# Ten-fold instead of eight-fold unrolling of the second edge loop of a two-layer graph network, on one core

## The reference

```python
src = edge_index[0]; dst = edge_index[1]               # layer 0: gated attention over all edges
attn = jax.nn.silu(jnp.sum(q[dst] * k[src] * dk, axis=1)) * _cosine_cutoff(edge_weight)
agg = jax.ops.segment_sum(v[src] * dv * attn[:, None], dst, num_segments=N)
...
key_e = k_rel[edge_type, edge_src]                     # layer 1: typed attention, 4 heads of 64
att = (q[edge_dst] * key_e).sum(-1) * rel_pri[edge_type] / sqrt(dk)
seg = edge_dst * r + edge_type
ex = jnp.exp(att - segment_max(att, seg)[seg])
w = ex / segment_sum(ex, seg)[seg]
hsum = segment_sum(w[:, :, None] * val_e, seg)
...                                                    # mean over types, typed projection, skip, norm
```

## Time and profile before

| | us |
|---|---|
| median of 3 runs | 3775.6 (3765.82 to 3777.75) |
| the profiled execution | 3789.33 |
| its span on the core | 3787.5 |
| second edge stage in it | about 1770 to 3450 |

### The profile page before, as it was taken

One profiled execution on the slowest core, in us unless ns is written; L12 is line 12 of the kernel. 1 busy time (PEld: TensorE's weight loads), 2 busy tenths in 40 slices (PEclk: granted clock), 3 DMA queues, 4 the chain that ended last, 5 costly groups with the idle time before them and its releaser, 6 DMA issues. The chain is left out here.

```text
span 3787.5 us, 113336 instructions
## 1 busy us (share of the span) xinstructions
PE 3442.8 (91%) x25474; PEld 2765.5 (73%) x25475; DVE 3283.3 (87%) x10411; ACT 2816.1 (74%) x8685; POOL 2448.1 (65%) x2605
## 2 busy tenths in 40 slices
PE   3978999999999997996999999999999999997997
PEld 2547777777777775774777777777777777776986
DVE  6768999999999995664899998999999999996775
ACT  2856777777777774553889888889889998885553
POOL 2656777777777773554566666666666666663776
PEclk8989999999999998998899999999999999998998
DMA  3879999999999994776888887888888888875664
GB/s 107 255 225 303 296 298 299 298 299 299 294 299 298 295 263 158 262 261 220 234 234 236 236 227 218 231 230 235 230 226 237 236 236 233 231 228 149 214 204 134
DMA packets 613511, 915.39 MB, mean 242 GB/s; under 512 B 210712, under 2 KB 422794, under 8 KB 612916
## 3 DMA queue, kind: packets, MB, share of 16 engines
q0 software_dynamic: 168160, 579.41, 47.9%
q1 hardware_dynamic: 445268, 335.07, 31.9%
HBM read 739.98 MB, written 177.47 MB: 242 GB/s over the span
## 5 line engine op out<-in xcount | busy, mean ns | idle before, releaser
L905 POOL DMA_INDIRECT kv<-kv_table,rec x864 | 887.5, 1027 | 293.6 <-issue 269.9
L1572 POOL DMA_INDIRECT kv1c<-kv_table,rec x912 | 877.4, 962 | 285.4 <-issue 262.4
L1617 ACT ACTIVATE wv<-kv1c,wv 128x64 f32<-128x64 f32 x3648 | 904.0, 334 | 16.0
L1680 DVE CUSTOM_DVE_ANT_0 masked_scores<-score_p,far 126x384 f32<-126x384 f32 x1216 | 604.6, 553 | 62.7 <-issue 28.5
L943 ACT ACTIVATE gates<-gates_p 128x512 f32<-128x512 f32 x864 | 465.5, 591 | 78.9 <-PE gates_p L1074 76.6
L1772 PE MATMUL sum_p<-wv,hot 128*126 128x260 f32 x1824 | 519.7, 424 | 2.3 <-ACT wv L1617 2.3
L1737 PE MATMUL qe_p<-qrel,hotT 126*128 126x256 f32 x1824 | 464.9, 392 | 26.1 <-ACT hotT L1602 18.0
L1094 PE MATMUL sum_p<-msg,hot_weighted 128*126 128x256 f32 x1728 | 432.2, 393 | 5.3 <-ACT hot_weighted L951 5.3
L1737 PEld LDWEIGHTS qe_p<-qrel,hotT 126*128 126x128 f32 x1824 | 363.8, 200 | 88.2 <-ACT hotT L1602 19.3
L1772 PEld LDWEIGHTS sum_p<-wv,hot 128*126 128x126 f32 x1824 | 339.8, 200 | 86.6 <-issue 3.8
L1582 POOL TENSOR_TENSOR faded<-acc,fade 126x260 f32<-126x260 f32 x304 | 189.2, 622 | 329.6 <-ACT fade L1625 324.1
(11 more groups left out here) (285 smaller groups left out, 7230.6 us busy)
## 6 DMA issues: line engine op xcount, KB each, us to landing
key<-segment_keys SPq DMA_DIRECT2D x304, 189.0 KB
q_blk<-q_table SPq DMA_DIRECT2D x216, 256.5 KB
acc_table<-acc SPq DMA_DIRECT2D x304, 128.0 KB
qrel<-q_by_relation SPq DMA_DIRECT2D x304, 126.0 KB
feat<-in_edge_feat_t SPq DMA_DIRECT2D x216, 128.0 KB
agg_and_x_plus_h<-total SPq DMA_DIRECT2D x216, 126.0 KB
kv1c<-kv_table,rec POOLq DMA_INDIRECT x912
kv<-kv_table,rec POOLq DMA_INDIRECT x864
```

The costliest lines, as they stand in the source:

```text
L905: pool.indirect_dma_start(kv[it.slot(AHEAD)][:, t, :], None, c["kv0_d"], bass.IndirectOffsetOnAxis(ap=rec[k][:, t, 0:1].bitcast(I32), axis ...
L1572: pool.indirect_dma_start(kv[k][:, t, :], None, c["kv1_d"], bass.IndirectOffsetOnAxis(ap=rec[k][:, t, 0:1].bitcast(I32), axis=0)).then_inc ...
L1617: ins = act.activation(wv[k][:, t, h, 0:DK], kv[s][:, t, D + h * DK:D + (h + 1) * DK], ACT.Copy, scale=wv[k][:, t, h, DK:DK + 1])
L1680: dve.tensor_tensor_reduce(junk[k][:, h], score_p[:, :, h, :], far[it.slot(4)][:], 1.0, -BIG, ALU.subtract, ALU.max, top[s][:, h:h + 1]).t ...
```

## The change

The loop of `edges_1` gets an unrolling of its own, U1 = 10, and `run_chunks` takes the unrolling as an argument; `edges_0` passes U = 8 as before. Everything in `edges_1` that was U deep is now ten deep, everything four deep is now five deep (`DEEP1`), and every wait for a free buffer looks back ten or five chunks in place of eight or four. The lags and the order of the stage functions stay. Two iterations are still written out ahead of the loop, which are now 20 chunks. `prepare` divides the chunk count by ten with a multiplication by 6554 and a shift by 16. The weights of `nodes_1` now live in a scope that closes before `w2` is allocated, so that their space is free for the deeper buffers.

```diff
+U1, DEEP1 = 10, 5
...
-def run_chunks(eng, steps, stages):
+def run_chunks(eng, steps, stages, unroll):
...
-    for s in range(2 * U):
+    for s in range(2 * unroll):
...
     with eng.Fori(2, steps) as i:
-        for u in range(U):
+        for u in range(unroll):
             for lag, f in stages:
-                f(Item(i, u - lag, U))
+                f(Item(i, u - lag, unroll))
...
+        with ExitStack() as middle:
+            def hold_w1(name, shape):
+                return middle.enter_context(nc.sbuf_tensor(name, shape, F32))
...
+            edges_0(nc, c)
+
+            nc.clear_and_free_semaphores(nc.allocated_since(before))
+            nc.all_engine_barrier()
+            nodes_1(nc, c)
...
-                link(dve.tensor_scalar(total_i[:], total[:], float(U - 1), None, ALU.add))
-                link(dve.tensor_scalar(total_i[:], total_i[:], U.bit_length() - 1, None, ALU.arith_shift_right))
+                dve.tensor_scalar(total_i[:, 0:1], total[:, 0:1], float(U - 1), None, ALU.add)
+                link(dve.tensor_scalar(total_i[:, 1:2], total[:, 1:2], float(U1 - 1), None, ALU.add))
+                link(dve.tensor_scalar(total_i[:, 1:2], total_i[:, 1:2], float((1 << 16) // U1 + 1), None, ALU.mult))
+                dve.tensor_scalar(total_i[:, 0:1], total_i[:, 0:1], U.bit_length() - 1, None, ALU.arith_shift_right)
+                link(dve.tensor_scalar(total_i[:, 1:2], total_i[:, 1:2], 16, None, ALU.arith_shift_right))
...
-        rec = [sb(f"rec1{k}", [P, T1, 4]) for k in range(U)]
+        rec = [sb(f"rec1{k}", [P, T1, 4]) for k in range(U1)]
...
-        kv = [sb(f"kv1c{k}", [P, T1, 2 * D]) for k in range(U)]
-        far = [sb(f"far{k}", [SEG, T1, P]) for k in range(4)]
+        kv = [sb(f"kv1c{k}", [P, T1, 2 * D]) for k in range(U1)]
+        far = [sb(f"far{k}", [SEG, T1, P]) for k in range(DEEP1)]
...
-                    wait(sp, acc_ready, it, U)
+                    wait(sp, acc_ready, it, U1)
...
-                    if isinstance(it.i, int) and it.index == U:
+                    if isinstance(it.i, int) and it.index == U1:
...
-                run_chunks(sp, steps, ((0, load), (7, store)))
+                run_chunks(sp, steps, ((0, load), (7, store)), U1)
...
-                    wait(pool, wv_ready, it, U)
+                    wait(pool, wv_ready, it, U1)
...
-                    wait(act, top_ready, it, 4, per=HEADS)
+                    wait(act, top_ready, it, DEEP1, per=HEADS)
...
-                    wait(act, of_edge_ready, it, 4)
+                    wait(act, of_edge_ready, it, DEEP1)
...
-                for k in range(U):
+                for k in range(U1):
                     dve.memset(peak[k][:], 0.0)
                     dve.memset(acc[k][:], 0.0).then_inc(filled, 1)
```

More of the change, by code:

```diff
@@ L150, in run_chunks @@
             if e < lag:
[L151 removed]
+                f(Item(steps, e - lag, unroll))
 def halves(ap):
@@ L885, in store @@
                     sp.dma_start(c["agg_xh_d"][ds(b * GROUP, GROUP), 0:D], total[k][:]).then_inc(stored, 16)
-                run_chunks(sp, steps, ((0, load), (6, store)))
+                run_chunks(sp, steps, ((0, load), (6, store)), U)
                 sp.wait_ge(stored, Item(steps, -1, U).count(per=16))
@@ L908, in gather @@
                         ).then_inc(gathered[k], 16)
-                run_chunks(pool, steps, ((0, gather),))
+                run_chunks(pool, steps, ((0, gather),), U)
             @block.scalar
@@ L1096, in sum_messages @@
                     ins.then_inc(msg_summed, 1)
-                run_chunks(pe, steps, ((1, edge_gates), (3, sum_messages), (1, q_of_edges), (0, turn)))
+                run_chunks(pe, steps, ((1, edge_gates), (3, sum_messages), (1, q_of_edges), (0, turn)), U)
 def nodes_1(nc, c):
@@ L1465, in edges_1 @@
         junk = [sb(f"masked_scores{k}", [SEG, HEADS, T1, P]) for k in range(2)]
[L1466 to L1470, removed]
+        top = [sb(f"top{k}", [SEG, HEADS]) for k in range(U1)]
+        old = [sb(f"old{k}", [SEG, HEADS]) for k in range(U1)]
+        peak = [sb(f"peak{k}", [SEG, HEADS]) for k in range(U1)]
+        drop = [sb(f"drop{k}", [SEG, HEADS]) for k in range(U1)]
+        fade = [sb(f"fade{k}", [SEG, HEADS]) for k in range(U1)]
         diff = [sb(f"diff{k}", [P, T1, HEADS]) for k in range(2)]
@@ L1474, in edges_1 @@
         faded = [sb(f"faded{k}", [SEG, HEADS, DK + 1]) for k in range(2)]
-        acc = [sb(f"acc{k}", [SEG, HEADS, DK + 1]) for k in range(U)]
+        acc = [sb(f"acc{k}", [SEG, HEADS, DK + 1]) for k in range(U1)]
         qe_p = ps("qe1_p", [P, 4, D])
@@ L1501, in _ @@
                     "blk", "k_in", "first", "n", "at", "row", "later", "done"))
-                used = [sp.alloc_register(f"used1{k}") for k in range(U)]
+                used = [sp.alloc_register(f"used1{k}") for k in range(U1)]
                 sp.reg_mov(blk, 0)
@@ L1553, in store @@
                                  ).then_inc(stored, 16)
-                run_chunks(sp, steps, ((0, load), (7, store)))
-                sp.wait_ge(stored, Item(steps, -1, U).count(per=16))
+                run_chunks(sp, steps, ((0, load), (7, store)), U1)
+                sp.wait_ge(stored, Item(steps, -1, U1).count(per=16))
                 sp.sem_inc(held, 1)
@@ L1583, in fade_acc @@
                         "s (h o) -> s h o", o=1).to_broadcast([SEG, HEADS, DK + 1]), ALU.mult).then_inc(faded_ready, 1)
-                run_chunks(pool, steps, ((5, fade_acc), (0, gather)))
+                run_chunks(pool, steps, ((5, fade_acc), (0, gather)), U1)
             @block.scalar
@@ L1621, in fades @@
                 def fades(it):
-                    s = it.slot(U)
+                    s = it.slot(U1)
                     wait(act, drop_ready, it)
-                    wait(act, faded_ready, it, U)
+                    wait(act, faded_ready, it, U1)
                     act.activation(fade[s][:], drop[s][:], ACT.Exp).then_inc(fade_ready, 1)
@@ L1640, in _ @@
                 dve.memset(zeros[:], 0.0).then_inc(filled, 1)
-                for k in range(4):
+                for k in range(DEEP1):
                     dve.memset(lanes[k][:], 0.0).then_inc(filled, 1)
@@ L1646, in one_hot @@
                 def one_hot(it):
-                    s = it.slot(U)
+                    s = it.slot(U1)
                     wait_slot(dve, loaded, it, LOADS)
-                    wait(dve, summed, it, U)
+                    wait(dve, summed, it, U1)
                     dve.scalar_tensor_tensor(hot[s][:],
@@ L1664, in scores @@
                     wait(dve, qk_ready, it)
[L1665 to L1666 removed]
+                    wait(dve, diff_ready, it, DEEP1)
+                    dve.tensor_reduce(score[it.slot(DEEP1)], qk[it.slot(2)][:], AX, ALU.add).then_inc(score_ready, 1)
                 def maxima(it):
[L1670 removed]
+                    k, s = it.slot(2), it.slot(U1)
                     wait(dve, spread_ready, it)
@@ L1719, in add_acc @@
                     wait(dve, faded_ready, it)
-                    wait(dve, stored, it, U, per=16)
-                    dve.tensor_tensor(acc[it.slot(U)][:], faded[it.slot(2)][:], sum_p[:], ALU.add).then_inc(acc_ready, 1)
+                    wait(dve, stored, it, U1, per=16)
+                    dve.tensor_tensor(acc[it.slot(U1)][:], faded[it.slot(2)][:], sum_p[:], ALU.add).then_inc(acc_ready, 1)
                 run_chunks(dve, steps, ((2, q_times_k), (3, old_peak), (4, below_peak), (2, scores), (4, cap),
-                                        (3, maxima), (5, add_acc), (3, new_peak), (0, one_hot), (3, peak_drop)))
+                                        (3, maxima), (5, add_acc), (3, new_peak), (0, one_hot), (3, peak_drop)), U1)
             @block.tensor
@@ L1761, in peaks_of_edges @@
                     for t in range(T1):
-                        ins = pe.matmul(peak_p[:, t, :], hotT[k][:, t, :], peak[it.slot(U)][:],
+                        ins = pe.matmul(peak_p[:, t, :], hotT[k][:, t, :], peak[it.slot(U1)][:],
                                         start=True, stop=True)
```

82 lines of the change are left out of this document (39 added, 43 removed).

## The result

| | us |
|---|---|
| median after, 5 runs | 3878.58 (3864.17 to 3886.27) |
| median before, 5 runs beside it | 3777.75 |
| ratio | 1.0252, 95% interval 1.0227 to 1.0276 |
| span of the profiled execution | 3884.5 (before 3787.5) |

A forecast was written before the change was run, and what follows sets the result against it. VectorE was taken to set the second edge stage's pace. The loop at 1494.1 to 1507.8 us, plus 24.2 written out and 0.5 small, saved 35 to 21 us; 30 off 3775.6 gave 3745.6 us, range 3718 to 3766.

The forecast's parts named there:

- The count of chunks: Second edge stage: 300 chunks are needed, so 304 become 300 and four idle chunks go.
- what ten deep buffers free: Second edge stage: nothing, as each relaxed wait has a stricter one ahead in its queue; at most 4.3 us.
- small: Ahead of the second edge stage: two added TENSOR_SCALAR with links, 0.5 us; five more fills, under 1 us, hidden.
- The sum: Second edge stage: 28 iterations take 1494.1 or 1507.8 us in place of 1553.8; 35 or 21 us less, 30 taken.
- the split between turn and chunk: Eight-fold loop: 2.36 us per iteration over eight plain chunks, 0.55 for the bare turn, 1.8 for turn or chunks.
- (2): Second edge loop: VectorE's longer body no longer stays and is fetched at each turn; 90 us, 3836 us; chance 0.12.
- No instruction packets in mid-loop: Sign to look for in the new profile's second edge loop: any such packets would mean VectorE's body is fetched anew.
- That row: Earlier profile's instruction-fetch rows: 55 packets of 8 KB, none from 2200 to 3400 us, so loop bodies stay.
- Its price: Refetch at each turn: 1.92 us of waiting and 1.3 us of lower clock, 3.2 per iteration, 90 us in all.
- the break in rows 8: Second eight written-out chunks in the earlier profile: TensorE waits 1.92 us for a peak, and the clock falls behind it.
- The clock drop behind it: TensorE after a refetch at the turn: lower clock, 1.3 us per iteration.

The follow-up runs named there:

- the kernel with the weights alone: The changed kernel with U1 = 8 and DEEP1 = 4, keeping only the giving back of the middle weights and the new count arithmetic: 3763.67 us, 0.9987.
- The four idle chunks alone: The kernel before with four more chunks written out, one iteration less in its eight-fold loop, 300 chunks: 3738.38 us, 0.9914; again 3733.71 us, 0.992.

## Why the prediction was wrong

*The count of chunks* held: 304 to 300. So did *what ten deep buffers free*: nothing; the sync queue still waits at `store`, for 290.3 us in the loop, and never at `load`. The first 20 chunks took 118.6 us, forecast about 119. The *small* parts are not to be seen in the kernel with the weights alone, though three TENSOR_SCALAR were added and not two.

*The sum* comes out where its premise, a body that stays, is met. In a good place the changed kernel is 29.5 us (70 idle instructions), 26.5 (45) and 25.2 (64) faster than the kernel before beside it, against 30 forecast, and takes 53.2 us per iteration against 53.5. That the total fits is in part luck, for its make-up was off. The four idle chunks alone, in the eight-fold kernel, give 32 and 31 us, which is all of the gain; the turns saved give nothing that can be seen. The mean iteration of 43.16 us came from an execution with a lower granted clock, 0.959 as a whole: the same loop in the kernel with the weights alone, at 0.966, took 42.67. So part of what I gave to the turn was that execution's share of clock drops, and the split between turn and chunk could not be read from a single execution.

The step that failed is the term for instruction fetch at the turn. *The sum* has none: 28 × (51.0 + 2.36) holds only if VectorE's body stays on the engine, and it did not; each of the 28 turns cost 4.95 us more, 139 us in all. That case stood among *the rivals*, as (2), and even its sign to look for ("No instruction packets in mid-loop; if there are any, rival (2) holds"). Its chance, 0.12, was set from the earlier trace rows, which shows only that bodies up to VectorE's 274 stay. That row says nothing of 340. I held the growth by a quarter for harmless without counting it against any size, though the packets' 8 KB stood in the same row, and a body's place in its packets can be counted in the program. The Trainium skill (Runtime: NRT & Kernel Launch, Instruction fetch mechanics) warned of just this, a branch back to a target that is no longer held. Its blocks of 256 instructions do not fit the fetches seen: single packets of 8 KB, five per iteration, the last ones 128 instructions apart. Its total of 512 is not contradicted, for three packets and one ahead are four times 128. Nor do the places tried rule out by themselves two blocks of 256 that stay: if the edge between 40 and 45 idle instructions is a block's as well, the starts are 213, 233 and 253 where the changed kernel was slow and 2, 21 and 27 where it was fast, 220 and 253 for the eight-fold one, and just the slow ones reach past 512.

*Its price* was too low: 3.2 us per turn, read off one break in the written-out chunks, against 4.95 measured (58.16 − 53.21), and 8.2 to 8.5 where the body starts three instructions ahead of a packet's end. The term that was mis-sized is the wait itself. Against the kernel with 70 idle instructions VectorE waits (117.1 − 8.7)/27 = 4.0 us more per iteration at the body's first operation (4.48 in the turn shown), where the break in rows 8 was 1.92; why that one was shorter is not shown. The clock drop behind it (1.46 us more for six matmuls, forecast 1.3) was sized well: VectorE's waits for TensorE's products grow by (66.2 − 24.4)/27 = 1.5 us per iteration. The remaining 0.6 us goes the other way. With 4.95 the rival would have said 3746 + 28 × 4.95 = 3884; the median was 3878.58.

## What to carry to other kernels

Before unrolling a loop further, count each engine's instructions in the body, waits and register work among them, and where the body starts in the stream. Where it reached into a fourth fetch packet of 128 here, each turn paid a fetch, and then a low clock on TensorE. The place mattered as much as the length, so an edit ahead of a loop, down to a few instructions, can switch the cost on or off; look for instruction packets in mid-loop in every profile. And where a loop's unrolling rounds the work up, writing a few steps more out ahead of it removes the idle ones without a longer body: here that gave the whole gain (3738.38 and 3733.71 us), with no filler.

## What was unexpected of the hardware

- VectorE's loop bodies come in packets of 128 instructions (8 KB each). Bodies that touched three were never fetched again (274 and 340 instructions); those that touched four were fetched in whole, five packets per iteration with the one ahead, also when the fourth held only 15 of their instructions (the eight-fold kernel with 33 idle ones). No other instruction packets were seen in mid-loop, so the bodies of TensorE (some 920 instructions by the trace's records of the changed kernel), ScalarE (246) and the sync queue (251) stayed; how long they may be was not tried.
- One such turn costs 4.95 us where the body starts 43 instructions ahead of a packet's end, 5.4 us where it starts 23 ahead, and about 8.4 us where it starts three ahead. Five idle instructions that are executed once can so be worth over 200 us: 3741.4 us with 45, 3960.8 with 40.
- What remains open: whether the packet ahead is what makes four too many, and whether a body of 340 that starts between 45 and 84 is fetched anew, as three packets of 128 would have it. The second wait grows as the first packet holds fewer of the body's instructions: none at 43, 0.75 us at 23, 3.9 us at three (medians, the last in the kernel with 40 idle instructions).
